# Last norm's residual formed by GpSimd and VectorE instead of TensorE, in a graph network layer with attention

## The reference, cut to what matters

```python
h = maximum(_layernorm(x), 0)                    # x: (8, 1024, 128)
x = x + _L0_gnn_ref(adj, h, W, b)                # max over up to 25 neighbours, a linear layer, relu
h = maximum(_layernorm(x), 0)
x = x + _L1_gnn_ref(h, adj, ...)                 # masked attention, 8 heads of 16, then:

    x = _layernorm(x + attn_out, ln1_g, ln1_b)   # n * ln1_g + ln1_b, n the normalized rows
    ff = relu(x @ W1.T + b1) @ W2.T + b2         # 512 hidden units
    x = _layernorm(x + ff, ln2_g, ln2_b)
```

## Time and profile before

| what | value |
|---|---|
| median of 3 runs | 1903.05 us (1896.24 to 1905.88) |
| profiled execution, its own time | 1908.26 us |
| its span, first to last instruction | 1906.5 us |
| instructions | 30090 |
| busy shares | PE 66%, ACT 42%, DVE 41%, POOL 38% |
| mean granted TensorE clock | 0.809 |

### The profile page before, as it was taken

How to read it: one execution, slowest core, us unless ns; L and a number is a source line. 1 busy time by engine, 2 the same in 40 slices (tenths; PEclk the granted TensorE clock), 3 DMA queues, 4 the chain that set the end, 5 groups by cost and what they waited for, 6 DMA issues and landing times.

```text
span 1906.5 us, 30090 instructions
## 1 busy us (share of the span) xinstructions
PE 1248.9 (66%) x11425; PEld 491.6 (26%) x11486; DVE 777.8 (41%) x3039; ACT 809.9 (42%) x1032; POOL 733.2 (38%) x743
## 2 busy tenths in 40 slices
PE   0144553676783657596585955867575977899985
PEld 0022210132231223232232312313122322343433
DVE  7566455152580536345360633615330231331323
ACT  1121342263543445274351734525342634678652
POOL 5655335724354435605445142633437043300000
PEclk8567776687896879698786977969686987999997
DMA  7432252322242222412223221422213211210000
GB/s 217 144 87 79 62 141 89 79 84 67 88 140 62 63 81 74 115 58 63 88 100 82 68 79 55 139 63 67 54 35 86 72 30 49 69 64 14 7 7 11
DMA packets 104518, 144.51 MB, mean 76 GB/s; under 512 B 17992, under 2 KB 77136, under 8 KB 104336
## 3 DMA queue, kind: packets, MB, share of 16 engines
q1 hardware_dynamic: 68352, 62.67, 10.6%
q0 software_dynamic: 22816, 44.61, 9.9%
q10 hardware_dynamic: 13168, 34.88, 5.3%
HBM read 124.79 MB, written 12.85 MB: 72 GB/s over the span
## 4 chain that ended last, share of the span: by engine, by line
PE 44%; another core or an unknown queue 21%; ACT 13%; issue 11%; DVE 9%; DMA 1%; DVEq 0%; ACTq 0%
PE sc L1526 14%; ACT probs L1307 11%; PE cb L1546 9%; PE sc L1530 7%; PE m L1616 2%; PE m L1603 2%; PE m L1428 1%; DVE cand L736 1%; PE m L1460 1%; DVE keys L732 1%; PE m L1643 1%; PE sc L1568 1%; PE m L1652 1%; PE m L1614 1%
## 5 line engine op out<-in xcount | busy, mean ns | idle before, releaser
L1307 ACT ACTIVATE probs<-sc 128x1024 f32<-128x1024 f32 x512 | 500.1, 1022 | 733.1 <-remote 494.4
L608 POOL DMA_INDIRECT nb_low<-h_rows,lsorted x474 | 473.6, 999 | 723.5 <-DVEq L911 563.4
L1546 PE MATMUL cb<-probs,va 128*17 128x512 f32 x2048 | 342.1, 645 | 40.7 <-issue 38.4
L1526 PE MATMUL sc<-q_near,k_g 32*128 32x512 f32 x1024 | 162.3, 705 | 132.8 <-ACT probs L1307 110.6
L1526 PE MATMUL sc<-q_far,k_g 32*128 32x512 f32 x1024 | 168.1, 694 | 117.2 <-ACT probs L1307 92.1
L1530 PE MATMUL sc<-barred,negident 32*32 32x512 bf16 x4096 | 166.4, 412 | 74.1 <-issue 71.6
L902 DVE TENSOR_REDUCE agg<-nb_low 128x128 f32<-128x1024 f32 (+6 forms) x64 | 114.1, 1783 | 40.9 <-issue 22.4
L1530 PEld LDWEIGHTS sc<-barred,negident 32*32 32x32 bf16 x4096 | 44.2, 89 | 324.5 <-issue 324.5
L673 DVE BATCH_NORM_STATS2 st<-m 128x6 f32<-128x128 f32 x64 | 14.2, 285 | 256.9 <-PE m L1616 208.5
L736 DVE MAX8 cand<-keys 128x8 f16<-128x128 f16 x512 | 105.3, 278 | 3.8 <-remote 1.7
L1299 ACT ACTIVATE barred<-m 128x512 bf16<-128x512 f32 x128 | 74.3, 606 | 74.1 <-issue 35.0
(11 more groups left out here) (186 smaller groups left out, 1620.1 us busy)
## 6 DMA issues: line engine op xcount, KB each, us to landing
adj_t<-in_adj_dram SPq DMA_DIRECT2D x64, 512.0 KB
adj_m<-in_adj_dram ACTq DMA_DIRECT2D x64, 512.0 KB
nb_low<-h_rows,lsorted POOLq DMA_INDIRECT x474
xh<-in_x_dram SPq DMA_DIRECT2D x8, 512.0 KB
h_rows<-xh SPq DMA_DIRECT2D x8, 512.0 KB
hl<-h_rows SPq DMA_DIRECT2D x8, 512.0 KB
x<-in_x_dram SPq DMA_DIRECT2D x16, 256.0 KB
out_dram<-h2T SPq DMA_DIRECT2D x16, 256.0 KB
```

The costliest lines, as they stand in the source:

```text
L608: pool.indirect_dma_start(out=dst, out_offset=None, in_=h_rows[0:(f + 1) * (N + 1), :], in_offset=bass.IndirectOffsetOnAxis(ap=lsorted[:, ...
L1307: nc.scalar.activation(probs[:, i % 2, 2 * pair:2 * pair + 2, :], sc[:, 2 * pair:2 * pair + 2, :], ACT.Exp, scale=SCALE).then_inc(s_probs, 1)
L1526: nc.tensor.matmul(sc[:, a, :], k[part, :], q[part, :], start=True, stop=False)
L1546: last = nc.tensor.matmul(cb[a * SPAN:a * SPAN + VW, :], va[:, u % 2, a, kt, :], probs[:, i % 2, a, :], start=(kt == 0), stop=(kt == T - 1))
```

## The change

GpSimd gets affine1(p): once TensorE has turned the normalized rows y of graph p, it multiplies y by ln1_g and adds ln1_b + b2, both in place over 128x1024, as two operations with a semaphore between them. It stands behind beta2 at tile 6 (at tile 5 for f = 2), and after the loop for graphs 6 and 7, for graph 7 by halves. forward loses the bias product and the diagonal products; its first w2 product of a tile opens the sum. finish first waits for GpSimd's result, then adds the bank to y in place with one VectorE operation, which frees the bank, and takes statistics and the scaled output from y. The rows ln1_g and ln1_b are loaded broadcast to all partitions (one DMA more), diag1 and a third of the bias tiles go away, `left` shares the space of aggx, and the semaphore prod_ready is merged into largest.

```diff
-L0B, BO, B12 = range(3)
-G2, B2R = range(2)
+L0B, BO = range(2)
+G2, B2R, G1, B12 = range(4)
...
-        diag1 = sb("diag1", [P, C])
-        bias_t = sb("bias_tiles", [P, 3, C], bf16)
-        rows = sb("bias_rows", [P, 2, C])
+        bias_t = sb("bias_tiles", [P, 2, C], bf16)
+        rows = sb("bias_rows", [P, 4, C])
...
-        left = sb("left", [P, 2, CHUNKS * 8], fp16)
...
+        left = aggx[:, :].bitcast(fp16)[:, 0:16 * CHUNKS].rearrange("p (a k) -> p a k", a=2)
...
+                def affine1(p, halves=((0, T),)):
+
+                    for j, (lo, hi) in enumerate(halves):
+                        v = y[:, lo:hi, :]
+                        done = 2 * p + 2 * j
+                        pool.wait_ge(s_nT_ready, 2 * p + hi // TH)
+                        nc.gpsimd.tensor_tensor(v, v, rows[:, G1:G1 + 1, :].to_broadcast([P, hi - lo, C]), ALU.mult).then_inc(s_y_based, 1)
+                        pool.wait_ge(s_y_based, done + 1)
+                        nc.gpsimd.tensor_tensor(v, v, rows[:, B12:B12 + 1, :].to_broadcast([P, hi - lo, C]), ALU.add).then_inc(s_y_based, 1)
...
                             beta2(f - 1)
+                        if t == (T - 3 if f == 2 else T - 2) and f >= 2:
+                            affine1(f - 2)
...
                 beta2(B - 1)
+                affine1(B - 2)
+                affine1(B - 1, ((0, TH), (TH, T)))
...
-                    ch.link(nc.vector.tensor_tensor(stage_rows[:, B12, :], stage_rows[:, B12, :], stage_b2, ALU.add))
+                    ch.link(nc.vector.tensor_tensor(rows[:, B12, :], rows[:, B12, :], stage_b2, ALU.add))
...
-                    ch.link(nc.vector.tensor_scalar(diag1[:, :], identf[:, :], g1c[:, 0:1], None, ALU.mult))
...
-                    def ffn(t):
-                        return m[:, h, t % TH * C:(t % TH + 1) * C]
+                    dve.wait_ge(s_y_based, 2 * p + 2 + (2 * h if p == B - 1 else 0))
                     dve.wait_ge(s_ffn_ready, 2 * p + h + 1)
-                    moments(ffn, st4, mv4, tiles)
+                    nc.vector.tensor_tensor(y[:, k, :], y[:, k, :], m[:, h, :].rearrange("p (t c) -> p t c", t=TH), ALU.add).then_inc(s_ffn_used, 1)
+                    dve.wait_ge(s_ffn_used, 2 * p + h + 1)
+                    moments(lambda t: y[:, t, :], st4, mv4, tiles)
...
                     for t in range(*tiles):
-                        nc.vector.tensor_scalar(y2[:, t, :], ffn(t), nw4[:, 4, t:t + 1], nw4[:, 3, t:t + 1], ALU.mult, ALU.add).then_inc(s_ffn_used, 1)
-                    dve.wait_ge(s_ffn_used, T * p + (h + 1) * TH)
+                        ch.step(nc.vector.tensor_scalar(y2[:, t, :], y[:, t, :], nw4[:, 4, t:t + 1], nw4[:, 3, t:t + 1], ALU.mult, ALU.add))
+                    ch.settle()
...
-                    for j, v in ((G2, ln2_g), (B2R, ln2_b)):
+                    for j, v in ((G2, ln2_g), (B2R, ln2_b), (G1, ln1_g), (B12, ln1_b)):
...
-                    for j, v in ((L0B, L0_b), (BO, bo), (B12, ln1_b)):
+                    for j, v in ((L0B, L0_b), (BO, bo)):
...
                     if part == 0:
                         refill(half)
-                        bias_rows(half, B12)
...
-                        cols = slice((half * TH + t) * P, (half * TH + t + 1) * P)
-                        nc.tensor.matmul(o, turned[:, cols], diag1[:, :], start=False, stop=False)
                         for k in range(FC):
-                            last = nc.tensor.matmul(o, hid[:, k, t * P:(t + 1) * P], w2T[:, k, :], start=False, stop=(t == TH - 1 and k == FC - 1))
+                            last = nc.tensor.matmul(o, hid[:, k, t * P:(t + 1) * P], w2T[:, k, :], start=(k == 0), stop=(k == FC - 1))
...
-                    freed[half] = (s_ffn_used, T * p + (half + 1) * TH)
+                    freed[half] = (s_ffn_used, 2 * p + half + 1)
```

More of the change, by code:

```diff
@@ L231, in program @@
         stage_w1 = wstage[:, 2048:2560]
-        stage_rows = wstage[:, 2560:2944].rearrange("p (j c) -> p j c", j=3)
+        stage_rows = wstage[:, 2560:2816].rearrange("p (j c) -> p j c", j=2)
         bv_wide = wstage[:, 2944:3072]
@@ L237, in program @@
         list_rows = lst[:, :, :].bitcast(fp16)[:, :, 0:COUNT + 1]
-        stage_part = wstage[:, 3200:3584].bitcast(bf16).rearrange("p (k j c) -> p k j c", k=2, j=3)
+        stage_part = wstage[:, 3200:3456].bitcast(bf16).rearrange("p (k j c) -> p k j c", k=2, j=2)
         sc = ctx.enter_context(nc.psum_tensor("sc", [P, 4, HALF], fp32))
@@ L295, in program @@
         s_largest = sem("largest")
-        s_prod_ready = sem("prod_ready")
         s_flag_row = sem("flag_row")
@@ L325, in program @@
         s_x1b = sem("x1b")
+        s_y_based = sem("y_based")
         s_out_ready = sem("out_ready")
@@ L331, in program @@
         VA_LOADS = 16 * (2 * GROUP - 1)
-        W_LOADS = 16 * (1 + 3 + 1 + FC + 1 + 2 + 4 + 2 * 2 * GROUP + FC + 2 + 1)
+        W_LOADS = 16 * (1 + 3 + 1 + FC + 1 + 4 + 3 + 2 * 2 * GROUP + FC + 2 + 1)
         def live(g):
@@ L983, in products @@
                 def products(f):
-                    dve.wait_ge(s_largest, 4 * f + 4)
+                    dve.wait_ge(s_largest, 5 * f + 4)
                     ch.link(nc.vector.tensor_reduce(pmax[:, :], amax[:, :, :], AX.X, ALU.max))
                     ch.link(nc.vector.tensor_tensor(pmax[:, :], pmax[:, :], bqk_abs[:, :, 0], ALU.add))
-                    nc.vector.tensor_tensor(prod[:, :], pmax[:, 0:1], pmax[:, 1:2], ALU.mult).then_inc(s_prod_ready, 1)
+                    nc.vector.tensor_tensor(prod[:, :], pmax[:, 0:1], pmax[:, 1:2], ALU.mult).then_inc(s_largest, 1)
                 def flag(f):
@@ L1663, in projection @@
                         last.then_inc(s_qk_ready, 1)
-                    freed[bank] = (s_largest, 4 * f + j + 1)
+                    freed[bank] = (s_largest, 5 * f + j + 1)
                 setup()
@@ L1748, in _ @@
                                 value_rows(f)
-                                pe.wait_ge(s_prod_ready, f + 1)
+                                pe.wait_ge(s_largest, 5 * f + 5)
                                 refill(0)
```

## The result

The changed kernel takes 1893.34 us (median, 1877.61 to 1900.95); the kernel before, run beside it, 1899.86 us (1891.39 to 1908.21). The ratio is 0.9965, 95% interval 0.9949 to 0.9981: 6.5 us less, where 20.1 were forecast. That 0.35% is clear of zero by its interval, and inside the 0.5% that I had named as no difference that can be told; the range of 1868 to 1901 held the time. The profiled execution took 1889.01 us against 1908.26 of before. That pair differs by 19 us because one is a quick execution of its kernel (4 us under the median) and the other a late one (8 us over it): whoever compares the two traces alone finds the forecast confirmed.

A forecast was written before the change was run, and what follows sets the result against it. TensorE was taken to bound the steps holding the second feed-forward product. Stages 2 to 7 14.3, stage 1 5.4 and tail 0.4 summed to 20.1 us: 1903.05 to 1883.0 us, range 1868 to 1901.

The forecast's parts named there:

- The change on TensorE, 1.10 us a half: Feed-forward steps: each half loses a bias product and four diagonal products, 1.10 us; 13 halves give 14.3 us.
- The tail's 0.4 us: End of the kernel: four diagonal products fewer, one VectorE add more, cheaper scalings; net win 0.4 us.
- I therefore let the win be kept: Stages with gather runs: VectorE and the next run follow TensorE, so time won outside the runs stays won.
- Rival 1, "Absorbed": Gather runs of stages 1 to 5 swallow TensorE's win ahead of them; 5.9 us left, 1897 us; chance 0.09.
- Stage 1, 5.4 us: Edge count's wait for bank 0 shrinks as the bank frees earlier: 5.4 us, both halves included; lower bound 2.2.
- the lower bound: Stage 1: 2.2 us is left if VectorE comes no earlier or the wait was already short.
- Stage 6, 2.2 us: Stage 6's two halves at normal pace, 1.10 us each, part of the 14.3 us for stages 2 to 7.
- GpSimd's 4.9 us, counted at nothing: affine1 ahead of tile 7's gather: 4.9 us a graph, covered by GpSimd's waits or counted as nothing in stage 5.
- The port, counted 0 with a bound of 14.2: Stages 2 to 4: affine1 may block first_norm's small VectorE operations, up to 4.7 us a stage; counted 0, bound 14.2.
- the low end of the range: 1868 us: affine1's break shortens TensorE's still time by 4.9 us in each of stages 2 to 4, 14.7 us.

The follow-up runs named there:

- d4: Changed kernel without GpSimd's two operations and without the gathers of graphs 2 to 7, against the kernel before: 1303.45 us, ratio 0.9931.
- b3: Changed kernel with ScalarE's mask tiles moved to other steps (12 and 16 freed), against the kernel before: 1915.00 us, ratio 0.9977.
- a1: Changed kernel without GpSimd's two operations and VectorE's wait for them, against the kernel before: 1911.70 us, ratio 0.9963.
- a2: Kernel before without the feed-forward's bias and diagonal products, finish unchanged, against the kernel before: 1910.16 us, ratio 0.9959.
- e2: a1's kernel run again on another chip, against the kernel before: 1884.78 us, ratio 0.9957.
- e3: e2's kernel plus twelve small chained VectorE instructions ahead of tile 7's wait in stages 2 to 5; against the kernel before: 1886.65 us, ratio 0.9950.
- the d pair: d4 against the kernel before without the gathers of graphs 2 to 7: 1303.45 against 1317.94 us, 14.5 us less.
- b4: Changed kernel unchanged, run again on b3's chip, against the kernel before: 1910.73 us, ratio 0.9955.
- c1: Kernel before plus affine1's two GpSimd operations, result unread, and finish's wait for them, against the kernel before: 1321.47 us, ratio 1.0057.
- d1: Changed kernel unchanged, on the fast chip, against the kernel before at 1313.23 us: 1313.98 us, ratio 1.0008.
- a4: Changed kernel with affine1 moved from ahead of tile 7's gather to between the last two sends, against the kernel before: 1916.09 us, ratio 0.9973.

## Why the prediction was wrong

- **The change on TensorE, 1.10 us a half: right in size.** It shows as 3.1 us for three halves in stage 7, as 4.39 and 4.41 us for the steps, and as 14.5 of the 20.1 us where nothing interferes (d4). The tail's 0.4 us came as 0.5 there, from the last exponential to the end.
- **"I therefore let the win be kept": this step failed.** It was argued from waits in the second half of a stage, and most of the feed-forward sums lie ahead of the large run. There the run's start is VectorE's, and ScalarE starts again some 5 us after its end (4.8 to 5.7 us in stages 2 to 4 of all traces with the hold, but for 6.7 in one stage of the changed kernel and 3.4 in one of b3), wherever TensorE was. Of a graph's 2.2 us only the products behind the run (step 16, 0.44 us) count in full; the 1.76 us ahead (half 0 and the first part of half 1) count if they complete a step, and else not at all. By their ratios a1, a2 and e2 have 7.1, 7.9 and 8.2 us left of 20.1. That the products' lead is lost at the large run is read from the traces; the experiments show that it is lost, and that a delay of VectorE ahead of the run is not paid for either (e3).
- **Rival 1, "Absorbed", 5.9 us, had this mechanism** and the measured size, with a chance of 0.09. I held against it that the other runs of a stage follow TensorE. They do, but the win is gone before them. What it did not have are the whole steps: with runs that simply keep VectorE's time, e3 would have been 14 us slower than e2. That its number fits the changed kernel is in part luck: it counted stage 6, where the changed kernel wins nothing (next points), and nothing from stages 1 to 5.
- **Stage 1, 5.4 us.** The wait went as forecast (4.72 to 1.95), and the d pair shows 3.0 us, between the lower bound and the term. On the chips with the hold stage 1 scatters from 217 to 223 us over the kernels without the products; one and the same kernel takes 222.5 (a1) and 217.4 (e2).
- **Stage 6, 2.2 us:** 1.4 in the d pair, 1.0 to 1.3 in a1, a2 and e2. Steps 12 and 16 take 4.9 to 5.7 us there (6.0 once, in b4) instead of 4.4, and step 16 4.9 to 5.4 us without the hold too. I suspected ScalarE's mask tiles; b3 did not bear it out, and it stays open.
- **GpSimd's 4.9 us, counted at nothing.** With the hold, about right in stages 2 to 4. In stage 6 affine1 shows: 155.6 and 156.9 us with it against 153.4 to 154.2 without. Stage 5 is 232.2 and 237.1 against 229.7 to 233.3, which the scatter doesn't part. Without the hold it was wrong: 7.5 us (c1), through the port and, as d1's rows have it, the late gather of tile 7.
- **The port, counted 0 with a bound of 14.2.** In stages 2 to 4 one instruction a stage is caught, for some 2.1 us more, and the large run comes 2.0 us later for it. Against that stands the step gained in affine1's break, which the low end of the range had priced at 4.9 us a stage for three stages. So GpSimd's part gives a step in stages 2 to 4 and takes it back through the port, the later run and the late gather of stage 6: b4 is 7.6 and a1 6.9 us faster than before by their medians, each on its own chip. In b4's stage 2 the step was lost again at the large run (step 16 behind it, 228.3 us), in stages 3 and 4 it was kept (222.7, 222.6). That the two sides cancel is read from these traces. a4 comes nearest to a test: its affine1 makes no break ahead of tile 7's gathers, its large run starts 36.4 to 37.2 us behind the first scatter, step 16 follows the run in all three stages, and it is 4.4 us slower than a1 on the same chip by the medians (1.9 us by the ratios, with intervals that overlap). So it has the delay without the step, and is slower, but not clear of noise.

## What to carry over

A win is worth what it is on the last resource that sets its stretch: find for each stretch between two fixed events (here gather runs placed by VectorE) who sets its length, and price the win there, not on the engine that is busiest. Where engines stand still for a length that somebody else fixes, time ahead of that place comes in whole units of work; a small win there is nothing or a whole step, and two single traces can differ by three times the true effect (here 19 us for 6.5). Slack that was measured beside such a standstill is slack only while the standstill is there.

## What the runs showed of the hardware

One kernel took 1895 to 1919 us on three chips and 1313 to 1315 us on a fourth, each within about 1% over its runs. Where the difference lies in the traces is TensorE's and ScalarE's standstill beside runs of indirect gathers: 88 matmuls against 381 in 38 us, with the gathers themselves some 1.25 us apart in both. On the slower chips the matmuls of one score step start 1.4 to 2.8 us apart in such a run, and ScalarE's wait is put down to nothing in the program ("issue", "remote"). Its cause is not settled. A hint that no run followed up: in e2 queue 8, one of the two DMA queues that carry instructions, moved nothing from 1222 to 1260 us, beside the large run, and in d1 it moved four packets of 16 KB in the 38 us beside the large run; whether that is a cause or follows from the standstill is open. A VectorE instruction on 128x8 values beside GpSimd's 2.36 us operations took 2.28 us, and in c1 5.23 us beside two of them, against 0.17.
